# Down products by slot instead of by channel in the experts, and set keys summed from tail keys

## The chip, the cores and the metric

One NeuronCore of a Trainium2 chip runs the kernel. The metric is the device time of one execution in microseconds, the median of several. TensorE (PE) multiplies matrices, VectorE (DVE), ScalarE (ACT) and GpSimd (POOL) work on vectors, SyncE (SP) issues most transfers. A transfer that is indexed by rows, or that adds to memory, is issued by GpSimd.

## The reference

4096 tokens (4 x 1024) of 256 channels, all float32, pass through:

```python
x = x + 0.5 * ffn(layernorm(x))        # quantised kernel and a LoRA pair
x = x + set_attention(layernorm(x))    # below
x = x + 0.5 * ffn(layernorm(x))
x = x + 0.5 * moe(layernorm(x))        # below
x = x + linear_attention(layernorm(x))
x = x + 0.5 * moe(layernorm(x))
```

Set attention has 16 heads. Its keys are sums over dyadic sets of 4, 8, 16, ... tokens (512 sets with the padding of this kernel) and, for each query, the tail: the sum of the keys from the last multiple of four up to the query itself. Values are summed alike:

```python
K = k_cum[r_idx] - k_cum[l_idx - 1]           # sets of 4, 8, 16, ...
K_tail = k_cum[t] - k_cum[t - t % 4 - 1]      # 1 to 4 tokens
logits = [q @ K.T * scale (where t >= r_idx), sum(q * K_tail) * scale]
```

The MoE has 32 experts, each taking its 160 best tokens (slots) among those that have it in their top two, and 16 adapters, one for two experts:

```python
idx = argsort(-score, axis=0)[:160].T
gate, up = split(xf[idx] @ w_up.T)            # 2 x 512 of 256
ye = (silu(gate) * up) @ w_down.T             # 256 of 512
out = zeros.at[idx].add(w * ye)
# the adapter of the expert's pair: 2 x 128 of 256, then 256 of 128, times 0.05 * w
```

## The kernel before

The change touches two places: the front of the set attention, and the expert loops of both MoEs, which share their code (`moe1e`, `moe2e` in the names of tiles).

**Attention front** (`attention_front`, line 507). It works batch by batch. `tailT` holds the running sums of four tokens of the normalised x, made by GpSimd; `setT` holds the sums over the 512 sets, made by VectorE in `sets` by one reduction over four tokens and then level by level (L635 to L641). TensorE then runs, in this order: the queries (four groups), the turning of the next batch, the tail keys `u_kt` (four groups of 512), the tail values, the set keys `u_k` from `setT` (two groups of 512, L724 to L727), the set values `u_v`, and the logits of the tails `u_tl` from `prod`. VectorE multiplies tail keys by queries into `prod` (L666) and splits queries and keys into three bf16 parts each (`split`, L650 to L655), which SyncE writes to `q_parts` and `k_parts`. ScalarE brings every other bank out of PSUM, among them the set keys into `kT`.

**Experts** (`experts`, line 2201). Four experts are a quad, two quads a turn, four turns a MoE. The first two turns carry steps of the choice of tokens for the second half of the experts. A quad's 640 slots lie in five tiles of 128 rows: tile k for k < 4 has the first 128 slots of expert k, tile 4 the last 32 of all four. `ORDER` is the order in which TensorE, ScalarE and VectorE go through a turn; n counts its eight experts, i the five pairs of 128 gate and 128 up channels (four of the expert, one of the adapter):

- x: ten transposes of the gathered rows in three groups (`TWO`), each copied to `xgT` by ScalarE; up 0 waits for all three.
- up(n, i): four matmuls, weights stationary, 160 slots moving (L2383). ScalarE takes silu (L2436), VectorE the product into `h` (L2507), two experts deep.
- down(n), after up(n + 1): for each half of the channels five matmuls, `w_down` stationary and 160 slots of `h` moving (L2396). The result has channels on the partitions; ScalarE copies it to `yT` (L2443, L2444). All downs use bank 5.
- y: ten transposes turn `yT` to rows of slots (L2364), in three groups, those of the first quad among the ups of the next, the last two of the second quad at the turn's end. ScalarE multiplies by the slots' weights into `y` (L2462).

The profile counts each f32 matmul as two instructions; a transpose is one.

GpSimd gathers x of the quad after next (L1348) and then adds `y` to the token rows in memory (L2328). A token can be in two experts of a quad, but at most once per phase, so a quad is stored in two phases: five stores with `first`, a wait until they have landed, five with `second`. In the last quad tiles 0 and 1 are stored alone (`whole`), each landed before what follows; then three tiles in two phases.

SyncE loads the weights: `w_up[k]`, `w_down[k]` and adapters k // 2 have one buffer for each k of a quad. Expert n + 4's `w_up` is loaded after up(n), its `w_down` after down(n), an adapter pair's two tiles after the down of an odd n.

## Time and profile before

| | us |
|---|---|
| median of 3 runs (1768.47 to 1768.91) | 1768.47 |
| the profiled execution | 1774.75 |
| its span, first to last instruction | 1773.0 |
| TensorE busy (share of the span) | 1468.0 (83%) |
| VectorE, ScalarE, GpSimd busy | 975.0, 719.1, 563.5 |
| experts of MoE 1, TensorE: first up to last y | 805.2 to 1111.7 |
| experts of MoE 2, TensorE: first up to last y | 1443.5 to 1750 |
| attention front | 67 to 213 |
| mean granted TensorE clock | 0.905 |

Starts are in us from the span's start. [...]

### The profile page before, as it was taken

To read this page: it belongs to the slowest core of one execution; us is meant where nothing else is said; L and a number is where in the kernel's file an instruction comes from. 1 tells how busy PE (TensorE), PEld (TensorE's weight loads), DVE (VectorE), ACT (ScalarE), POOL (GpSimd) and SP (SyncE) were. 2 spreads that over 40 slices of the span, in tenths; PEclk is the share of its full clock that TensorE was granted. 3 is DMA by queue.
4 is the path that set the end of the run, shared out by engine and by line. 5 is a ranking of instruction groups with operands and counts; after the bars stand their busy time and mean duration, and the time that the engine had idled before them with its cause. 6 is when DMAs were issued, how large, how long until landed. Compare 5 with 4: busy or idle time off the path is not lost. (4 is left out here: it accounts for less than half of the span.)

```text
span 1773.0 us, 27014 instructions
## 1 busy us (share of the span) xinstructions
PE 1468.0 (83%) x9520; PEld 1131.4 (64%) x9520; DVE 975.0 (55%) x2816; ACT 719.1 (41%) x1744; POOL 563.5 (32%) x467
## 2 busy tenths in 40 slices
PE   6899979999999678438999999289895469999994
PEld 4566644555555455228889989166563349899994
DVE  8775577787875487874441111256675945521110
ACT  4223137666666377325523333004333435322331
POOL 6522120000000343303536563421211231636545
PEclk9989889999999899558999999699996569999997
DMA  3034373424220023314869995501113226979974
GB/s 105 18 119 127 109 123 65 91 42 93 42 47 2 1 84 107 140 31 151 246 183 261 239 241 133 137 20 48 48 43 135 72 79 205 228 230 232 267 194 46
DMA packets 113764, 212.10 MB, mean 120 GB/s; under 512 B 20101, under 2 KB 79658, under 8 KB 104426
## 3 DMA queue, kind: packets, MB, share of 16 engines
q1 hardware_dynamic: 87338, 178.93, 32.6%
q0 software_dynamic: 26304, 31.60, 11.6%
q8 instruction: 69, 1.13, 0.3%
q14 instruction: 53, 0.43, 0.1%
HBM read 158.71 MB, written 51.38 MB: 118 GB/s over the span
## 5 line engine op out<-in xcount | busy, mean ns | idle before, releaser
L952 DVE TENSOR_REDUCE attnm_top<-psum 128x1 f32<-128x384 f32 (+3 forms) x384 | 212.9, 597 | 59.8 <-PE psum L1037 55.7
L1174 ACT ACTIVATE attnm_prob<-psum 128x512 f32<-128x512 f32 (+1 forms) x384 | 192.1, 530 | 91.0 <-PE psum L1047 84.4
L2507 DVE SCALAR_TENSOR_TENSOR moe2e_h<-moe2e_gate,psum 128x160 f32<-128x160 f32 x160 | 50.4, 320 | 201.1 <-ACT moe2e_gate L2436 165.6
L2507 DVE SCALAR_TENSOR_TENSOR moe1e_h<-moe1e_gate,psum 128x160 f32<-128x160 f32 x160 | 50.4, 321 | 200.5 <-ACT moe1e_gate L2436 179.0
L2328 POOL DMA_INDIRECT x_sum<-moe1e_y,moe_scatter_i x76 | 119.4, 1571 | 129.4 <-ACT moe1e_y L2462 70.7
L2328 POOL DMA_INDIRECT out<-moe2e_y,moe_scatter_i x76 | 118.8, 1563 | 129.9 <-ACT moe2e_y L2462 69.8
L2383 PE MATMUL psum<-moe2e_xgT,moe_w_up 128*128 128x160 f32 x1024 | 152.3, 304 | 2.5 <-ACT moe2e_xgT L2452 1.9
L2383 PE MATMUL psum<-moe1e_xgT,moe_w_up 128*128 128x160 f32 x1024 | 152.4, 304 | 2.4 <-ACT moe1e_xgT L2452 1.9
L2383 PEld LDWEIGHTS psum<-moe2e_xgT,moe_w_up 128*128 128x128 f32 x1024 | 144.4, 193 | 4.8 <-issue 4.8
L2383 PEld LDWEIGHTS psum<-moe1e_xgT,moe_w_up 128*128 128x128 f32 x1024 | 144.4, 193 | 4.8 <-issue 4.8
L1348 POOL DMA_INDIRECT moe_xg<-xn_rows,moe_gather_i x80 | 83.9, 1049 | 159.2 <-DVE moe_gather_i L1536 93.0
L938 POOL TENSOR_TENSOR attnm_tail_v<-attnm_v_tail,attnm_tail_p 128x256 f32<-128x256 f32 x32 | 19.8, 620 | 346.5 <-PE psum L1089 284.5
L1035 PE MATMUL psum<-attn_mask_ts,ident_bf 128*128 128x128 bf16 x512 | 106.3, 227 | 9.1 <-DVE attnm_top L952 6.9
L1037 PE MATMUL psum<-attnm_k_hat,attnm_q_hat 96*128 96x512 bf16 (+3 forms) x384 | 107.4, 308 | 0.0
L1047 PE MATMUL psum<-attnm_q_hat,attnm_k_hat 99*128 99x512 bf16 (+1 forms) x288 | 98.4, 345 | 1.4 <-ACT attnm_prob L1174 0.6
L2436 ACT ACTIVATE moe1e_gate<-psum 128x160 f32<-128x160 f32 x160 | 47.2, 301 | 104.9 <-PE psum L2383 98.1
L2436 ACT ACTIVATE moe2e_gate<-psum 128x160 f32<-128x160 f32 x160 | 47.2, 301 | 104.9 <-PE psum L2383 92.2
L2396 PE MATMUL psum<-moe2e_h,moe_w_down 128*128 128x160 f32 x512 | 80.3, 300 | 2.1 <-ACT moe2e_yT L2444 1.2
L2396 PE MATMUL psum<-moe1e_h,moe_w_down 128*128 128x160 f32 x512 | 80.3, 300 | 2.1 <-issue 1.5
L1035 PEld LDWEIGHTS psum<-attn_mask_ts,ident_bf 128*128 128x128 bf16 x512 | 51.0, 101 | 46.2 <-issue 24.5
L1060 PE MATMUL psum<-attnm_prob,attn_v_aug 128*32 128x512 f32 (+1 forms) x768 | 78.7, 527 | 0.0
L1045 PE MATMUL psum<-attn_mask_st,ident_bf 128*128 128x256 bf16 x256 | 70.4, 277 | 5.4 <-DMA attn_q_first<-attnm_mT 5.3
(416 smaller groups left out, 3198.8 us busy)
## 6 DMA issues: line engine op xcount, KB each, us to landing
moe_w_up<-in_expert_up SPq DMA_DIRECT2D x64, 1024.0 KB
moe_w_down<-in_expert_down SPq DMA_DIRECT2D x64, 512.0 KB
attnm_q_hat<-q_parts SPq DMA_DIRECT2D x72, 128.0 KB, 4.7
moe_a_up<-in_adapter_up SPq DMA_DIRECT2D x32, 256.0 KB
q_parts<-attnf_q_part SPq DMA_DIRECT2D x12, 512.0 KB, 2.8
attnm_k_hat<-k_parts SPq DMA_DIRECT2D x72, 64.0 KB, 2.3
x_res<-in_x SPq DMA_DIRECT2D x8, 512.0 KB, 8.4
v_tails<-attnf_v_tail SPq DMA_DIRECT2D x4, 1024.0 KB, 4.3
```

The costliest lines, as they stand in the source:

```text
L952: nc.vector.tensor_reduce(top[:, n // QUADS % 2, tiles[0]:tiles[-1] + 1, hh:hh + 1], s.ps[:, u.bank, 0:len(tiles) * width].rearrange("p (t ...
L1035: nc.tensor.matmul(out[:, width - P:width], s.identb[:], o.mask_ts[:, tile % 2, :], start=(i == 0), stop=False, skip_group_check=True)
L1037: ins = nc.tensor.matmul(out, q_hat[r][0:MROW, h, tile * P:(tile + 1) * P], k_hat[r][0:MROW, h, 0:width], start=False, stop=True, skip_gro ...
L1047: nc.tensor.matmul(s.ps[:, u.bank, at:GROUP], k_hat[r][0:MROW + NPART, h, j * P:(j + 1) * P], q_hat[r][0:MROW + NPART, h, g * GROUP + at:( ...
L1060: ins = nc.tensor.matmul(s.ps[32 * h:32 * h + 32, u.bank, at:GROUP], o.v_aug[:, first:first + 32], prob[:, i % NPROB, at:GROUP], start=(j ...
L1174: nc.scalar.activation(prob[:, i % NPROB, at:GROUP], s.ps[:, u.bank, at:GROUP], ACT.Exp).then_inc(taken[u.bank], 1)
L1348: pool.indirect_dma_start(self.xg[:, q, k, :], None, self.rows, bass.IndirectOffsetOnAxis(ap=self.gather_i[:, at:at + 1], axis=0), bounds_ ...
L2328: nc.gpsimd.indirect_dma_start(total, bass.IndirectOffsetOnAxis(ap=rows, axis=0), y[:, q, k, :], None, bounds_check=TOKENS + SPARE - 1, oo ...
L2383: ins = nc.tensor.matmul(s.ps[:, u.bank, half * CAP:(half + 1) * CAP], lhsT, xgT[:, q, c, k * CAP:(k + 1) * CAP], start=(c == 0), stop=(c ...
L2396: ins = nc.tensor.matmul(s.ps[:, u.bank, o * CAP:(o + 1) * CAP], lhsT, h[:, n % 2, i, :], start=(i == 0), stop=(i == PAIRS - 1))
L2436: nc.scalar.activation(gate[:, i, :], s.ps[:, u.bank, 0:CAP], ACT.Silu).then_inc(silu, 1)
L2507: nc.vector.scalar_tensor_tensor(out=h[:, n % 2, i, :], in0=gate[:, i, :], scalar=1.0 if i < INTER // P else SCALE_A, in1=s.ps[:, u.bank, ...
```

## The change

*Front.* The product of the set keys is dropped. VectorE copies every fourth tail key, which is the sum of its four tokens, out of the PSUM bank from which it has just made `prod`, and builds the larger sets from these with the same additions as for `setT` (now the function `larger`).

*Experts.* The down product has the first 128 slots of `h` stationary and the 256 channels of `w_down` moving, five matmuls for an expert, and leaves rows of slots in PSUM; ScalarE weighs them at once into `y`. The last 32 slots of a quad's four experts are multiplied in `tails`, ahead of the quad's last down: 20 matmuls with 32 stationary columns each, expert k into partitions 32k to 32k + 31 of one bank. `yT` and its turns are gone; `h` is five experts deep. x comes in the groups (0, 4), (1, 2), (3), placed among the pairs of up 0. SyncE loads a quad's four `w_down` and two `a_down` after that quad's last down; `w_up` follows up(n), `a_up` its last pair. Quads 0 to 6 are stored in two phases as before; in the last one tiles 0, 1 and 2 are stored whole, each landed before the next, then the tail tile and tile 3 in two phases.

```diff
-                for f in range(CC):
-                    mm_group(u_k[b, f], [(s.ps[:, u_k[b, f].bank, :], lambda c: wk[:, c, f * P:(f + 1) * P],
-                                          lambda c: setT[:, z, c].rearrange("p j i -> p (j i)"))])
...
                         nc.vector.tensor_tensor(prod[:, f, g * GROUP:(g + 1) * GROUP], s.ps[:, u.bank, :],
-                                                qT[:, z, f, g * GROUP:(g + 1) * GROUP], ALU.mult).then_inc(taken[u.bank], 1)
+                                                qT[:, z, f, g * GROUP:(g + 1) * GROUP], ALU.mult)
+                        of_four = s.ps[:, u.bank, :].rearrange("p (j i k) -> p j i k", j=SC // BG, k=4)[:, :, :, 3]
+                        ins = nc.vector.tensor_copy(k_sets[:, f, g * SC // BG:(g + 1) * SC // BG, 0:64], of_four)
+                        ins.then_inc(taken[u.bank], 1)
+                v.wait_ge(taken[u.bank], u.after(0))
+                chain.link(larger(k_sets))
...
-TWO = [(0, 1), (2, 3), (4,)]
-ALONE = TWO[0]
+FETCH = [(0, 4), (1, 2), (3,)]
+TAIL = EQ
...
-    h = sb("h", [P, 2, PAIRS, CAP])
-    yT = sb("yT", [P, 2, CC, QE])
+    HELD = [0, 1, 2, 3, 4, 0, 1, 2]
+    h = sb("h", [P, EQ + 1, PAIRS, CAP])
...
         if n == 0:
-            ORDER += [("x", 0, None)] + [("up", 0, i) for i in range(PAIRS)]
+            ORDER += [("x", 0, 0)]
+            for i in range(PAIRS):
+                ORDER += [("up", 0, i)]
+                if i in (1, 3):
+                    ORDER += [("x", 0, (i + 1) // 2)]
         if n == 1:
-            ORDER += [("x", 1, None)]
+            ORDER += [("x", 1, i) for i in range(len(FETCH))]
         if n + 1 < 2 * EQ:
-            for i in range(PAIRS):
-                ORDER += [("up", n + 1, i)]
-                if n == EQ and i < len(TWO):
-                    ORDER += [("y", 0, i)]
-                if n == EQ + 2 and i == 0:
-                    ORDER += [("y", 1, 0)]
+            ORDER += [("up", n + 1, i) for i in range(PAIRS)]
+        if n % EQ == EQ - 1:
+            ORDER += [("tails", n // EQ, None)]
         ORDER += [("down", n, None)]
-    ORDER += [("y", 1, i) for i in range(1, len(TWO))]
...
+            def next_up(n):
+                if n < 2 * EQ and not (last and n >= EQ):
                     sp.wait_ge(full[u_up[n, INTER // P - 1].bank], up[n])
                     m.load_up(sp, t * 2 * EQ + n + EQ, n % EQ)
-                    sp.wait_ge(full[u_down[n].bank], down[n])
-                    m.load_down(sp, t * 2 * EQ + n + EQ, n % EQ)
                     if n % 2:
-                        m.load_adapter(sp, t * EQ + n // 2 + EQ // 2, n % EQ // 2)
+                        sp.wait_ge(full[u_up[n, PAIRS - 1].bank], a_up[n // 2])
+                        m.load_a_up(sp, t * EQ + n // 2 + EQ // 2, n % EQ // 2)
+
+            for q in range(2):
+                if last and q == 1:
+                    break
+                first = 0 if q == 0 else EQ + 2
+                for n in range(first, EQ * q + EQ):
+                    next_up(n)
+                sp.wait_ge(full[u_down[EQ * q + EQ - 1].bank], down[q])
+                for k in range(EQ):
+                    m.load_down(sp, t * 2 * EQ + EQ * q + EQ + k, k)
+                    if k % 2 == 0:
+                        m.load_a_down(sp, t * EQ + (q + 1) * EQ // 2 + k // 2, k // 2)
+                    if q == 0 and k % 2:
+                        next_up(EQ + k // 2)
...
+            else:
+                for k in range(EQ - 1):
+                    done = store(k, whole[k])
+                    landed(done)
+                for rows in (first, second):
+                    for k in (TAIL, EQ - 1):
+                        done = store(k, rows[k])
+                    if rows is first:
+                        landed(done)
...
+        def down_weight(k, i):
+            return w_down[k][:, i, :] if i < INTER // P else a_down[k // 2][:]
...
-            for o in range(CC):
-                for i in range(PAIRS):
-                    if o == 0:
-                        pe.wait_ge(taken[u_up[n, i].bank], u_up[n, i].after(t))
-                    lhsT = w_down[k][:, i, o * P:(o + 1) * P] if i < INTER // P else a_down[k // 2][:, o * P:(o + 1) * P]
-                    ins = nc.tensor.matmul(s.ps[:, u.bank, o * CAP:(o + 1) * CAP], lhsT, h[:, n % 2, i, :],
-                                           start=(i == 0), stop=(i == PAIRS - 1))
+            for i in range(PAIRS):
+                pe.wait_ge(taken[u_up[n, i].bank], u_up[n, i].after(t))
+                ins = nc.tensor.matmul(s.ps[:, u.bank, 0:C], h[:, HELD[n], i, 0:P], down_weight(k, i),
+                                       start=(i == 0), stop=(i == PAIRS - 1))
+            ins.then_inc(full[u.bank], 1)
+
+        def tails(t, q):
...
+            for i in range(PAIRS):
+                last = u_up[EQ * q + EQ - 1, i]
+                pe.wait_ge(taken[last.bank], last.after(t))
+                for k in range(EQ):
+                    rows = slice((CAP - P) * k, (CAP - P) * (k + 1))
+                    ins = nc.tensor.matmul(s.ps[rows, u.bank, 0:C], h[:, HELD[EQ * q + k], i, P:CAP], down_weight(k, i),
+                                           start=(i == 0), stop=(i == PAIRS - 1), skip_group_check=True)
```

The index list `whole` is now made for both halves of the experts (in `lists`, two VectorE operations more for the first half).

## Rows read from the trace of the kernel before

**Rows 1.** Windows in MoE 1: busy us by engine, clock, DMA share, GB/s.

```profile
949.00:1019.00 70.00, 66.98 (x481) 65.60 (x480) 12.55 (x41) 21.57 (x67) 41.51 (x30) 0.98 0.92 244
...
1111.70:1134.70 23.00, 0.02 (x1) 0.00 (x0) 0.00 (x0) 1.04 (x3) 10.87 (x7) 0.58 0.36 40
```

**Rows 2.** The chain that ended last, second MoE: start us, us, what.

```profile
1628.62 5.43 PE psum L2383 x40
1634.05 2.72 PE psum L2396 x20
...
1745.49 3.00 PE psum L2396 x20
```

**Rows 3.** Timeline of TensorE, MoE 1: start us, us, what, [idle before <-releaser].

```profile
1024.97 0.60 PE L2364 MATMUL psum<-ident,moe1e_yT 128*128 128x128 f32 x4
1025.41 3.42 PE L2383 MATMUL psum<-moe1e_xgT,moe_w_up 128*128 128x160 f32 x24
...
1033.22 1.35 PE L2396 MATMUL psum<-moe1e_h,moe_w_down 128*128 128x160 f32 x8 [0.58 <-issue]
...
1036.85 0.87 PE L2364 MATMUL psum<-ident,moe1e_yT 128*128 128x128 f32 x6 [0.65 <-ACT moe1e_yT L2444]
...
1038.43 1.09 PE L2354 MATMUL psum<-ident,moe_xg 128*128 128x128 f32 x8 [0.71 <-ACT moe1e_y L2462]
...
1040.74 4.47 PE L2383 MATMUL psum<-moe1e_xgT,moe_w_up 128*128 128x160 f32 x31 [0.54 <-issue]
```

**Rows 4.** Timeline of GpSimd: stores under load, a gather, the end of MoE 2.

```profile
1024.61 1.55 POOL L2328 DMA_INDIRECT x_sum<-moe1e_y,moe_scatter_i  x1 [5.47 <-DMA x_sum<-moe1e_y,moe_scatter_i]
...
1035.29 1.05 POOL L1348 DMA_INDIRECT moe_xg<-xn_rows,moe_gather_i  x1 [0.31 <-issue]
...
1746.38 1.55 POOL L2328 DMA_INDIRECT out<-moe2e_y,moe_c_whole  x1 [3.17 <-DMA out<-moe2e_y,moe_scatter_i]
...
1767.26 1.55 POOL L2328 DMA_INDIRECT out<-moe2e_y,moe_scatter_i  x1 [0.30 <-issue]
```

**Rows 5.** Timeline of TensorE in the attention front.

```profile
162.47 7.07 PE L689 MATMUL psum<-attnf_w,attnf_tailT 128*128 128x256 f32 x32
169.38 3.60 PE L689 MATMUL psum<-attnf_setT,attnf_w 128*128 128x512 f32 x8
172.81 3.62 PE L689 MATMUL psum<-attnf_w,attnf_setT 128*128 128x256 f32 x16
```

**Rows 6.** Timeline of VectorE in the attention front.

```profile
182.78 1.66 DVE L635 TENSOR_TENSOR attnf_setT<-attnf_setT 128x256 f32<-128x256 f32 x6
...
206.48 0.69 DVE L650 CAST attnf_k_part<-attnf_kT 128x1024 bf16<-128x1024 f32 x1 [7.40 <-issue]
```

**Rows 7.** Value products of attention: groups by shape, then timeline of TensorE.

```profile
L1060 PE MATMUL psum<-attnm_prob,attn_v_aug 128*32 128x256 f32 x8 | 0.6, 379 | 0.0
...
447.32 0.38 PE L1047 MATMUL psum<-attnm_q_hat,attnm_k_hat 99*128 99x512 bf16 x1
447.54 0.60 PE L1081 MATMUL psum<-ident,attnm_oT 128*128 128x128 f32 x4
...
448.25 0.38 PE L1047 MATMUL psum<-attnm_q_hat,attnm_k_hat 99*128 99x512 bf16 x1
448.56 1.50 PE L1060 MATMUL psum<-attnm_prob,attn_v_aug 128*32 128x512 f32 x16
449.99 0.23 PE L1035 MATMUL psum<-attn_mask_ts,ident_bf 128*128 128x128 bf16 x1
```

**Rows 8.** DMA issues by line, then timeline of SyncE.

```profile
attnf_w<-in_attn_wqkv SPq DMA_DIRECT2D x1, 768.0 KB, 4.2
...
1036.23 0.33 SPq L1356 DMA_DIRECT2D moe_w_down<-in_expert_down  x1
```

**Rows 9.** Timeline of TensorE at the start of MoE 1.

```profile
799.85 1.12 PE L2354 MATMUL psum<-ident,moe_xg 128*128 128x128 f32 x4 [7.66 <-DMA moe_xg<-xn_rows,moe_gather_i]
...
805.22 6.02 PE L2383 MATMUL psum<-moe1e_xgT,moe_w_up 128*128 128x160 f32 x32 [0.66 <-ACT moe1e_xgT L2452]
```

More of the change, by code:

```diff
@@ L2308, in gather @@
             m.gather(pool, quad)
+        stored = itertools.count(1)
         def add(quad):
             q, t = quad % 2, quad // 2
+            choice, at = m.choices[quad // late.quads], quad % late.quads
+            whole = [choice.whole[:, at, k:k + 1] for k in range(EQ)]
             first, second = ([scatter_i[:, (quad * 2 + i) * ST_TILES + k:(quad * 2 + i) * ST_TILES + k + 1]
                               for k in range(ST_TILES)] for i in range(2))
-            phases = [list(enumerate(first)), list(enumerate(second))]
@@ L2317, in add, with store @@
-            if quad == QUADS_E - 1:
-                phases = [[(k, late.whole[:, late.quads - 1, k:k + 1])] for k in ALONE] + [of[len(ALONE):] for of in phases]
+            def store(k, rows):
+                u = u_tails[q] if k == TAIL else u_down[EQ * q + k]
+                pool.wait_ge(taken[u.bank], u.after(t))
+                nc.gpsimd.indirect_dma_start(total, bass.IndirectOffsetOnAxis(ap=rows, axis=0),
+                                             y[:, q, k, :], None, bounds_check=TOKENS + SPARE - 1, oob_is_err=True,
+                                             compute_op=ALU.add).then_inc(y_out, 16)
+                return next(stored)
```

212 lines of the change are left out of this document (101 added, 111 removed).

## The prediction

> **What bounds the kernel now.** I read the views in this order. First the windows of the expert stages: over a middle turn (two quads of four experts) TensorE is busy 66.98 of 70 us at clock 0.98, while the DMA engines are busy for 0.92 of the time and VectorE and ScalarE for less than a third; then come 23 us without TensorE [rows 1]. Second the chain that ended last: through the second MoE it is TensorE group after group, one expert's up product (5.43 us, L2383) and its down product (2.72 us, L2396) in turn; TensorE leaves it at 1745.49 + 3.00 = 1748.5 us [rows 2]. So an expert costs 8.15 us of TensorE and whatever shortens that, or the gaps between, shortens the stage. Third TensorE's timeline at a boundary between turns: it turns y (L2364), then x (L2354), and sits idle 0.58, 0.65, 0.71 and 0.54 us in between, 2.5 us a turn [rows 3]. Fourth GpSimd at the end of a MoE, which alone sets those 23 us: the last store is issued 18.8 us after TensorE's last product [rows 2, 4]. Fifth the attention front, where TensorE runs group after group without a gap [rows 5]. DMA is the second resource: not yet waited for, but with little room.
>
> **The profiled execution** took 1774.75 us with a span of 1773.0; the median of the three timed runs is 1768.47, 0.3% less. Savings are taken over at their size in us.
>
> **Front: set keys from the tail keys.** Removed per batch: the product L724-727, 8 instructions of 512 columns, from 169.38 to 172.81, 3.43 us [rows 5]. TensorE is the bound there, so four batches give 13.7 us; should the group of one batch lie in a stretch at half clock, it is worth twice as much, so up to 17. Added to VectorE: four strided copies out of PSUM and nine small sums. The six sums of the same shape take 1.66 us, the other four some 0.5; a copy is under 0.3, as 0.69 us is already paid for a 1024-element cast: together 3.4 us. Its cover is the 7.40 us that VectorE idles ahead of the key split [rows 6]. It now need not wait for the product at all, so the split starts at about 202.7 instead of 206.48. If the cover were gone, 3.4 us a batch would come back. ScalarE's two evacuations vanish, at no gain. **Front: -13.7 us** (-12 to -17).
>
> **One turn of the experts.** A product of 128 slots by 256 channels in f32 costs what the 32 instructions from 162.47 to 169.38 do: 6.91/32 = 0.216 us each [rows 5]. A down product by slot is five matmuls, ten instructions, 2.16 us against 2.72. Eight experts: -4.5. The turns of y go: four transposes take 1025.41 - 1024.97 = 0.44 us [rows 3], ten a quad 1.1, two quads: -2.2. The tails come in: 20 matmuls a quad of 32 stationary columns by 256. One after the other they would take 40 x 0.216 = 8.6 us, four column groups side by side 2.16. The row that decides is the value product of the attention, with the same 128x32 weights and the same 256 columns: eight instructions are busy for 0.6 us where eight in a row would take 1.7, and sixteen (half of 512 columns) pass from 448.56 to 449.99, 1.43 us, against 1.28 for perfect overlap and 5.1 for none [rows 7]. I take 2.16, two quads: +4.3. Work: -2.4 us a turn, -9.4 a MoE, 0.6 of it behind the last product.
>
> The groups of 32 columns are entered and left twice a turn. Before the value product the matmul of L1047 is followed after 0.31 us, elsewhere after 0.22 (0.09 more), and 1.43 - 1.28 = 0.15 remain on the way out [rows 7]: 0.24 a visit, eight visits: +1.9 a MoE. [...]
>
> Gaps: at a boundary the waits for the copies of y, for their bank, and for bank 5 go, the last because the tails stand between down 6 and down 7. Left is the copy of the first x group, now two ScalarE copies: some 0.9 us, and 0.3 in the second x. 2.5 becomes 1.2: -1.3 a turn, -5.2 a MoE. Banks 6 and 7 and the h slots hold nothing up: the slot written by up 5 was last read by down 0 and the tails.
>
> **The wait that is added.** All four w_down of a quad are read by its tails, so SyncE can load none until the quad's last down product is through; before, each was loaded with three experts' time to spare. Queued behind that wait on SyncE are the four w_down, two a_down and the next w_up. At a turn's end the cover is x and two ups, over 11 us. In the middle of a turn it is one up, 5.43 us [rows 2]. To be landed by then: 640 KB. The nearest row is a 768 KB load that lands in 4.2 us with the queue to itself, and issue costs 0.33 us a transfer [rows 8]; 0.33 + 0.5 for the second issue + about 4 = 5 us, just covered. But stores run then on GpSimd's queue; a landing that takes 3.2 us when quiet takes 5.5 us under load [rows 4], 2.3 more. The bounds are 0 and 3 us of stall; I take 1.0. Four times: +4 (0 to +12) a MoE.
>
> **Start of a MoE.** x tiles 0 and 4 are gathered first, and up 0 waits for these alone. Now TensorE turns the first two tiles at 799.85 and starts up 0 at 805.22, with 0.66 us for a copy [rows 9]. Afterwards: 799.85 + 0.5 + two copies and their signals, about 802.0. The other groups have landed by the second pair. **-3.2 us.** Two added VectorE operations in `lists` come after the gather indices, while TensorE waits 7.66 us for the first x [rows 9]: 0.
>
> **End of a MoE.** A store costs 1.55 + 0.30 us, a landing wait 3.2 (quiet) to 5.5 us after it [rows 4]. Before, from the last down product to the landing: 1767.26 + 1.55 + 3.0 - 1748.5 = 23.3 us. Afterwards I count from E, the end of quad 6; TensorE ends at E + 5.43 x 3 + 2.16 x 5 = E + 27.1, plus the stall and drain, E + 28.3. GpSimd: tile 3 and the tail of quad 6, first phase, landed at E + 7.3; five stores, landed at 19.5; tiles 0, 1 and 2 whole, one after another at 4.7 each, 33.6; two stores and landing 40.2; again, 46.9. So 18.6 us after TensorE instead of 23.3, -4.7; with landings under load in quad 6 some 2.3 less. I take **-4.0**. GpSimd, not TensorE, sets this part: three landings in a row cost more than they save in stores, and a TensorE that is earlier by 1 us gains nothing in the last quad alone.
>
> GpSimd's cycle: ten stores 18.6, five gathers 1.36 each [rows 4] 6.8, a landing 3.2 to 5.5: 28.6 to 30.9 us against 33.6 for half a turn. It holds, and y of a parity is free about 14 us before ScalarE wants it.
>
> **Sum** per MoE: start -3.2, work -9.4 + 0.6 = -8.8, visits +1.9, gaps -5.2, weights +4.0, end -4.0: -15.3. Two: -30.6. With the front: -44.3. 1768.5 - 44.3 = **1724 us**.
>
> **Rivals.** (A) *The weights give it back.* Landing late by 3 us or more in mid-turn, or the bunched loads make transfers of the first experts late elsewhere. For it: DMA share 0.92 in the middle turn [rows 1]. Against: averaged over the turn the bytes don't grow, and one up covers the quiet price. At 3 us, +8 a MoE over my term: 1740; with the end not gaining either, 1748. Chance 0.17. [...] (B) *Slower: the tails don't overlap*, because four different w_down tiles are streamed. Each quad then pays 8.6 instead of 2.16, 6.5 x 16 = +104: 1828. It decides above 2.16 + 44.3/16 = 4.9 us a quad. Against: in the value product each group has a moving operand of its own too and overlaps [rows 7]. Chance 0.04. (C) *No stall, and the clock holds.* The middle turns show a stretch below full clock after a boundary (0.98 over 70 us [rows 1], 1.4 us); with shorter gaps it may go, and the weights land in time: -8 -3: 1713; with a front of 17 and a full -4.7 at the end, 1708. Chance 0.17. (D) *GpSimd becomes the bound of the stage*: a landing of 5.5 us in both phases, and the gathers slowed by the bursts; 3 us a quad over half a turn in ten quads: 1754. Chance 0.03. Forecast, with its stalls of 0.3 to 2 us: 0.59, 1716 to 1736.
>
> **Range**: from C's lower end, less 2 us for what C itself leaves open, to A with a lost end: 1706 to 1748. A measurement of this kernel can tell 0.2% (3.5 us) from no change. Faster 0.95 (forecast, A, C, most of D), same 0.01, slower 0.04 (B).
>
> **What would show it.** Right: in the front no 512-column group of the set keys, and TensorE's period per batch 3.4 us less; down groups of ten instructions in 2.16 us; the tails' 40 instructions in 2.2 to 2.5 us; turns, from the first up product to the next turn's, shorter by 2.5 to 3.5 us; a gap on TensorE ahead of the first down product of a turn's second quad, released by the w_down load, of 0 to 2 us, and none ahead of other downs; three landings in a row in the last quad, and the last store issued about 14 us after TensorE's last product. Wrong: tails of 4 us or more (B), that gap over 3 us or gaps at other downs (A), GpSimd without an idle microsecond over a turn (D), or the key split on VectorE later than the products of TensorE that follow it.

## The result, and the profile of the changed kernel

The changed kernel took 1743.94 us (median of 4, 1737.69 to 1750.05), the kernel before beside it 1768.69 us (1768.47 to 1771.16): ratio 0.9861, interval 0.9833 to 0.9889, so 24.7 us or 1.4% faster. The forecast was 1724, 44.3 us faster. On three further occasions the same kernel took 1728.7, 1740.5 and 1724.5 us (below): how much it gains depends on the occasion, which the kernel before does not show.

**What came as told.** Timeline of TensorE in the changed kernel, end of the middle turn in MoE 2 and start of the next (start us, us, line, tiles, rows*columns, count, [idle before <-releaser]):

```profile
1627.77 1.67 PE L2427 MATMUL psum<-moe_w_down,moe2e_h 128*128 128x256 f32 x7
1629.28 0.59 PE L2427 MATMUL psum<-moe_a_down,moe2e_h 128*128 128x256 f32 x2
1629.80 1.93 PE L2441 MATMUL psum<-moe_w_down,moe2e_h 128*32 128x256 f32 x32
1631.55 0.61 PE L2441 MATMUL psum<-moe_a_down,moe2e_h 128*32 128x256 f32 x8
1632.10 1.99 PE L2427 MATMUL psum<-moe_w_down,moe2e_h 128*128 128x256 f32 x8
1633.93 0.59 PE L2427 MATMUL psum<-moe_a_down,moe2e_h 128*128 128x256 f32 x2
1634.36 0.60 PE L2394 MATMUL psum<-ident,moe_xg 128*128 128x128 f32 x4
1640.16 4.63 PE L2413 MATMUL psum<-moe2e_xgT,moe_w_up 128*128 128x160 f32 x16 [5.20 <-ACT moe2e_xgT L2490]
```

A down product passes in some 2.2 us (1632.10 to 1634.36 with the return from the column groups) where it took 2.72 [rows 2]. A listed duration can reach past the start of the group behind it (1631.55 + 0.61 = 1632.16, and the next starts at 1632.10), so I read paces from starts. The tails' 40 instructions pass in 2.30 us (1629.80 to 1632.10), 0.14 more than the 2.16 of four groups side by side: the groups overlap almost in full. Nothing of y is turned any more [rows 3].

**What came otherwise** is in the last row. TensorE idles 5.20 us before the first up of the turn, where I had counted on some 0.9. ScalarE and GpSimd in the same stretch:

```profile
1629.91 0.47 ACT L2501 ACTIVATE moe2e_y<-psum,moe2e_weight 128x256 f32<-128x256 f32 x1 [1.86 <-PE psum L2427]
1635.01 0.47 ACT L2501 ACTIVATE moe2e_y<-psum,moe2e_weight 128x256 f32<-128x256 f32 x1 [4.62 <-remote]
1637.91 0.47 ACT L2501 ACTIVATE moe2e_y<-psum,moe2e_weight 128x256 f32<-128x256 f32 x1 [2.43 <-remote]
1639.38 0.37 ACT L2492 COPY moe2e_xgT<-psum 128x256 f32<-128x256 f32 x1 [1.00 <-remote]
```

```profile
1629.99 1.09 POOL L1348 DMA_INDIRECT moe_xg<-xn_rows,moe_gather_i  x1 [0.31 <-issue]
...
1635.38 1.01 POOL L1348 DMA_INDIRECT moe_xg<-xn_rows,moe_gather_i  x1 [0.30 <-issue]
1636.69 1.62 POOL L2344 DMA_INDIRECT out<-moe2e_y,moe_scatter_i  x1 [0.30 <-issue]
```

By TensorE's records the tails were through at 1632.1, the last down at 1634.4 and the x turn at 1634.8. ScalarE, which did nothing else, took them up at 1635.01, 1637.91 and 1639.38: 2.9, 3.5 and 4.6 us later. The releaser is listed as "remote", the profile's word where no recorded instruction fits the signal. I call this a **late signal**. The profile's ends of TensorE's instructions are modelled, so the rows do not tell whether the signal was late or the product behind it. It falls in or just after the five gathers of GpSimd (1629.99 to 1636.39). The gap has a second price, in the windows of the same kernel (span, busy us of TensorE, its weight loads, VectorE, ScalarE, GpSimd; clock, DMA share, GB/s):

```profile
1632.00:1636.00 4.00, 2.96 (x18) 2.32 (x14) 0.00 (x0) 0.47 (x1) 3.09 (x4) 1.00 0.88 219
1636.00:1640.00 4.00, 0.00 (x0) 0.00 (x0) 0.00 (x0) 1.09 (x3) 3.39 (x3) 0.92 0.52 97
1640.00:1644.00 4.00, 3.84 (x14) 3.85 (x15) 0.32 (x1) 0.33 (x2) 3.31 (x3) 0.50 1.06 351
1644.00:1648.00 4.00, 4.00 (x24) 3.96 (x24) 0.64 (x2) 1.25 (x4) 1.55 (x1) 0.72 1.11 303
```

After the idle stretch the granted clock is 0.50 in each window of 2 us from 1640 to 1646, and 0.95 in the next: the first 16 up instructions are busy for 4.63 us instead of 2.44 (the same 16 at a granted clock of 1.00 on occasion D, below). Such a stretch at 0.50 is what I call half clock. So 4.4 us more of gap come with some 3 us more of work behind it.

The waits of ScalarE that end on "remote" add up to 51 us in the two MoEs of this profile (21 waits); in the kernel before they are 3.7 us (2 waits of 1.85). Most cost nothing, as TensorE runs on meanwhile. Those at a turn's start cost the gaps of 4.66 us (at 1485.57), 5.20 us (1640.16) and 2.00 us (1008.43). Beside them there are two stalls on `a_down`, 1.28 and 0.65 us; my term for the weights had 4 us a MoE.

One table goes through all that follows. From the timelines of TensorE I took for each MoE the stretch from the first x turn to the end of the last down product; from ScalarE's the sum of its waits on "remote"; the times are the medians. "Occasion" names the runs that were made side by side; B and D were made on one chip, C on another.

| Run | occasion | median us | profiled us | MoE 1 | MoE 2 | late signals, us | longest gap at a turn's start |
|---|---|---|---|---|---|---|---|
| before | A | 1768.7 | 1774.8 | 311.9 | 312.0 | 3.7 | 0.8 |
| changed | A | 1743.9 | 1737.7 | 295.7 | 308.3 | 51 | 5.20 |
| changed | B | 1728.7 | 1740.9 | 299.2 | 302.3 | 30 | 3.72 |
| changed | C | 1740.5 | 1741.9 | 302.0 | 302.1 | 41 | 5.24 |
| changed | D | 1724.5 | 1724.1 | 292.3 | 292.1 | 0 | 0.81 |

(In the kernel before, the stretch ends with the last turn of y, 1.5 us behind the last product.) The three profiles with late signals have stretches that sum to 601.5 to 604.1 us and took 1737.7 to 1741.9; the one without has 584.4 and took 1724.1. On occasion B only the profiled execution was so long; the other five took 1724.8 to 1729.5 us. A profile shows one execution, and a median is that of several, so times and stretches are best compared within the profiled executions.

### The profile page after: what moved, and what is told of

The parts are those of the page before. It is cut to its first block and busy times, and to the rows that moved or that the text cites. A ratio compares the mean times of both kernels' runs of the same rounds, so it can differ in the third digit from the quotient of the medians.

```text
span 1736.0 us, 26631 instructions
## 1 busy us (share of the span) xinstructions
PE 1433.7 (83%) x9328; PEld 1075.2 (62%) x9328; DVE 988.1 (57%) x2872; ACT 689.3 (40%) x1640; POOL 561.6 (32%) x465
## 5 line engine op out<-in xcount | busy, mean ns | idle before, releaser
L2413 PE MATMUL psum<-moe2e_xgT,moe_w_up 128*128 128x160 f32 x1024 | 154.3, 309 | 11.5 <-ACT moe2e_xgT L2490 6.0
L2413 PEld LDWEIGHTS psum<-moe2e_xgT,moe_w_up 128*128 128x128 f32 x1024 | 148.5, 197 | 14.8 <-issue 13.9
L87 DVE BATCH_NORM_STATS2 x_stats<-x_res 128x6 f32<-128x256 f32 x128 | 44.5, 412 | 36.1 <-DMA x_res<-x_sum 35.5
L2427 PE MATMUL psum<-moe_w_down,moe2e_h 128*128 128x256 f32 x256 | 62.1, 384 | 1.5 <-issue 0.9
```

What stands on the lines that cost most here:

```text
L2413: ins = nc.tensor.matmul(s.ps[:, u.bank, half * CAP:(half + 1) * CAP], lhsT, xgT[:, q, c, k * CAP:(k + 1) * CAP], start=(c == 0), stop=(c ...
L2427: ins = nc.tensor.matmul(s.ps[:, u.bank, 0:C], h[:, HELD[n], i, 0:P], down_weight(k, i), start=(i == 0), stop=(i == PAIRS - 1))
```

## The experiments

The runs are told in the order of the questions.

**The changed kernel again**, on occasion B, unedited.

> The changed kernel once more, beside the parts of it. In its first profile ScalarE waited 49.9 us in all for signals of TensorE that came 2 to 6 us after TensorE's own records of the products ended (3.8 us in the kernel before). If these late signals are what spreads its times (1737.7 to 1750.1), the time is 1738 to 1750 again, and an execution with more of them is a longer one. If they belong to that one profile only, the time is within 2 us of 1744 and this profile shows under 10 us of them.

Measured: 1728.72 us (1724.83 to 1740.85), ratio 0.978 (0.9762 to 0.9798). Neither of the two outcomes came. The one profiled execution, with 30 us of late signals, is the longest of the six.

**The front alone**, with the experts as before.

```
-        for f in range(CC):
-            u_k[b, f] = use()
...
+                chain.link(larger(k_sets))
```

> Only the front of the change, on the kernel before. My working gave -13.7 us (four groups of 3.43 us of TensorE), so 1755. If VectorE's added sums took the place of the product, or the clock's slow stretches moved, the gain is under 8 us, 1761 or more.

Measured: 1755.71 us (1751.51 to 1760.45), ratio 0.993 (0.9909 to 0.9951), beside 1768.25: -12.5 us, against -13.7. The 512-column group is gone, as TensorE's timeline of this run shows (it ran from 169.38 to 172.81 [rows 5]):

```profile
174.37 7.03 PE L696 MATMUL psum<-attnf_tailT,attnf_w 128*128 128x512 f32 x16
181.23 7.07 PE L696 MATMUL psum<-attnf_w,attnf_tailT 128*128 128x256 f32 x32
188.14 3.62 PE L696 MATMUL psum<-attnf_w,attnf_setT 128*128 128x256 f32 x16
191.59 3.63 PE L742 MATMUL psum<-attn_head_sum,attnf_prod 128*128 128x8 f32 x32
```

**The experts alone**, with the front as before (the rest of the diff).

> Only the experts' part. By my working -30.6 us (1738). By the first profile, in which the first MoE gained 14.8 us and the second 2.0 us and the end of neither MoE gained, it is 1750 to 1760. If front and experts add up, this gain and that of the front alone give the whole change's.

Measured: 1750.09 us (1739.12 to 1753.79), ratio 0.9904 (0.9886 to 0.9922): -18.2 us, against -30.6. The two parts give -30.7 together, the whole gave -39.5 on this occasion; 9 us are not additive, and why is not shown: this profile has 32 us of late signals, a gap of 5.12 us at 1643.02 and MoE stretches of 293.3 and 300.6 us, but it is that of the fastest of the seven executions (1739.12; the others took 1747.7 to 1753.8).

**The gather between the two phases of a quad**, in the wait for the landing of the first phase, so that no gather runs under the tails.

```
                     if rows is first:
+                        ahead(quad)
                         landed(done)
...
-            if quad + 2 < QUADS_E:
-                gather(quad + 2)
             add(quad)
```

> The changed kernel with one move: GpSimd issues the five gathers of the quad after next between the two phases of stores, inside the wait for the first phase's landing (8.3 to 9.8 us in middle turns), instead of ahead of the stores. Theory (gathers under way while the tails run hold TensorE's signals back, and GpSimd's backlog of 6.8 us a quad sets the end): no tails product overlaps a gather any more, late signals fall from 50 us to under 15, the first whole store of the last quad is no longer late, and the time falls by 8 to 16 us, to 1728 to 1736. Rival (the signals are late because of the bunched weight loads, or it is the landing of the stores alone that sets the end): late signals stay above 30 us and the time moves by less than 4 us.

Measured: 1765.43 us (1760.2 to 1773.26), ratio 0.9983, 37 us slower than the changed kernel beside it. The profile has no late signal, and something worse: TensorE waits for x at three turn starts of each MoE.

```profile
880.18 2.77 PE L2397 MATMUL psum<-ident,moe_xg 128*128 128x128 f32 x10 [4.82 <-DMA moe_xg<-xn_rows,moe_gather_i]
```

The others are 5.65, 6.51, 5.27, 4.32 and 4.75 us, each with a stretch of lower clock behind it (0.50 to 0.52 in its lowest window of 2 us); the MoE stretches are 312.6 and 312.3 us, 20 more than at the changed kernel's best. The cause is GpSimd's queue: the five gathers, now behind the quad's first five stores, ran from 871.41 to 878.04, and TensorE stood waiting from 875.36 on. I had held GpSimd to be free for 3 to 5 us in a quad. In the changed kernel (occasion D) GpSimd's waits for a landing were this long in a middle turn:

```profile
960.65 1.56 POOL L2344 DMA_INDIRECT x_sum<-moe1e_y,moe_scatter_i  x1 [3.72 <-DMA x_sum<-moe1e_y,moe_scatter_i]
...
994.49 1.55 POOL L2344 DMA_INDIRECT x_sum<-moe1e_y,moe_scatter_i  x1 [8.71 <-DMA x_sum<-moe1e_y,moe_scatter_i]
```

From one set of gathers to the next it is 28.9 and 33.8 us (941.11, 969.97, 1003.79): 25.4 us of stores and gathers, and a landing. A quad of TensorE takes 35.3. GpSimd is nearly full, as rival D had it, and just not the bound. The two waits differ although the DMA engines are as busy in both (share 1.07 and 1.08): in the shorter one they move 226 GB/s and in the longer one 348, behind the bunched `w_down` loads that SyncE issues from 978.86 on.

**The changed kernel, a third time** (occasion C), beside the three runs that follow.

> The changed kernel as it is, for the three that run beside it on the same chip. It gave 1743.9 us once and 1728.7 us on another occasion, with late signals of TensorE adding up to 50 and 30 us of waits. If these waits set the difference, the sum of the waits that end on a remote releaser in this profile goes with its time: about 30 us at 1725 to 1741 us, about 50 us at 1738 to 1750 us. If they are no cause, the time is anywhere in 1725 to 1750 us whatever the sum of these waits.

Measured: 1740.49 us (1738.58 to 1751.92), ratio 0.9858 (0.9812 to 0.9904), 41 us of late signals, and one gap of 5.24 us (1015.92) and one of 4.50 (1645.43). Behind the first the granted clock is 0.50 from 1015 to 1021, behind the second 0.50 from 1647 to 1649.

**Alternating kinds.** Every expert slot holds the first or the second pick of its token, so first picks never meet each other's rows, nor second picks theirs; only the two kinds must be kept apart. Odd quads therefore store their second picks first. The landing between quads goes, one a quad stays, and the gathers fill it. `free` waits for the other quad's stores and hands its y back. (The spare rows that empty slots are added to get a second set, and each parity of quads gets a semaphore of its own.)

```
-            landed(done)
...
-                for rows in (first, second):
+                for i, rows in enumerate((first, second) if q == 0 else (second, first)):
                     for k in range(ST_TILES):
+                        if i == 0 and k == ST_TILES - 1:
+                            free()
...
+                    if i == 0:
+                        ahead(quad)
+                        landed(q)
```

> Odd quads store second picks first and then first picks, so that the last phase of a quad and the first one of the next add rows of one kind and no landing lies between them; the gather for the quad after next stands between the two phases, in the landing wait, as in the run with the moved gather. Theory that GpSimd bounds the loaded turns: its work per quad was 10 stores of 1.86 us, 5 gathers of 1.35 us and a landing wait of 8.9 us, 34.3 us of a turn of some 35.5 us; now it is 18.6 + 6.8 + about 2 = 27.4 us. GpSimd then idles for some 5 to 8 us per quad until ScalarE has weighed a tile, x is there at every turn (no wait of 4 to 6 us as with the moved gather alone), the second to last quad's stores end before TensorE's last product and not 2 us after it, and the end from the last product to the last landing shrinks from 23.3 to about 20 us: 5 to 15 us faster than the changed kernel. Rival, GpSimd is beside the path all the time: GpSimd idles more, everything else stays, within 3 us of the changed kernel. Rival, a gather between the phases is bad for whatever reason: 15 us or more slower, as the moved gather alone was (+37 us).

Measured: 1731.80 us (1724.37 to 1734.92), ratio 0.9803 (0.9776 to 0.983), 8.7 us faster than the changed kernel beside it, within the 5 to 15 expected, and none of its five executions (up to 1734.92) is as long as the shortest of the changed kernel's four (1738.58). GpSimd now waits for work (timeline, MoE 1):

```profile
1027.14 1.55 POOL L2352 DMA_INDIRECT x_sum<-moe1e_y,moe_scatter_i  x1 [0.30 <-issue]
1033.09 1.55 POOL L2352 DMA_INDIRECT x_sum<-moe1e_y,moe_scatter_i  x1 [4.40 <-ACT moe1e_y L2509]
1040.68 1.55 POOL L2352 DMA_INDIRECT x_sum<-moe1e_y,moe_scatter_i  x1 [6.04 <-ACT moe1e_y L2509]
```

Late signals are 15 us, the gaps at turn starts 1.2 to 2.45 us (a little of x's lateness stays), and the stretches are 294.5 and 294.8 us against 302.0 and 302.1. The end did not shrink, against the expectation: the last store is issued 18.9 us after the last product. Nor does this run show a gain where there are no late signals: the stretches are 2.2 and 2.7 us longer than those of the changed kernel on occasion D.

**A quarter of the up weights**: is it the load of the transfers? The reloads bring 256 KB of each expert's 1 MB and leave the rest as it was, so the results are others.

```
-                    m.load_up(sp, t * 2 * EQ + n + EQ, n % EQ)
+                    m.load_part(sp, t * 2 * EQ + n + EQ, n % EQ)
...
+        sp.dma_start(self.w_up[k][:, :, 0:INTER // 2], self.drams[0][bass.ds(e, 1), :, :, 0:INTER // 2].rearrange(
+            "o p c j -> (o p) c j")).then_inc(self.up_in[k], 16)
```

> Every expert's up weights after the first quad are reloaded only in a quarter of their columns (256 KB and not 1 MB each), so that stale weights are used and the output is another; instructions and their order stay. Theory that the transfers' load makes stores land late and signals come late: landing waits in the middle turns fall from 8 to 10 us to the 3.1 us of the quiet end, no wait of ScalarE ends on a remote releaser for more than 1 us, and the time falls by 10 to 25 us against the changed kernel. Rival, the five gathers themselves hold the signals up: landing waits fall, but late signals of 2 to 6 us stay at the gathers, and the time falls by less than 10 us.

Measured: 1751.82 us (one execution), within the 1738.58 to 1751.92 of the changed kernel beside it; a fall by 10 to 25 us, which the theory asked for, did not come. Over 940 to 1010 the DMA share falls to 0.76 and 172 GB/s. The landing waits between two phases do not fall to the 3.1 us that I expected: they are 3.6 and 8.0 us in this stretch and 6.5 us in the mean of all 14 (3.6 to 9.9), against 7.6 us (3.7 to 10.0) in the changed kernel beside it. The late signals are 60 us (27 waits, up to 7.1) where they were 41, and four turns start with gaps of 4.74 to 5.57 us. So the bytes of the up weights account for a small part of the landings, and they are not what makes the signals late.

**Ten whole products in place of the tails**: is it the column groups?

```
-                for k in range(EQ):
-                    rows = slice((CAP - P) * k, (CAP - P) * (k + 1))
-                    ins = nc.tensor.matmul(s.ps[rows, u.bank, 0:C], h[:, HELD[EQ * q + k], i, P:CAP], down_weight(k, i),
+                for k in (EQ - 1,):
+                    ins = nc.tensor.matmul(s.ps[:, u.bank, 0:C], h[:, HELD[EQ * q + k], i, 0:P], down_weight(k, i),
```

> The tails of a quad, 40 products of 32 rows in four column groups (2.3 us), are replaced by one expert's 10 products of 128 rows (2.2 us), so the tail tile holds wrong rows. Theory that TensorE's column groups hold its own signals up: no late signal at the tails any more, TensorE's gaps at turn starts fall to 0.8 us, and the time falls by 5 to 15 us against the changed kernel. Rival, the late signals come from GpSimd's or the transfers' side: they stay at 20 us or more in all, and the time stays within 3 us of the changed kernel.

Measured: 1722.59 us (1719.15 to 1728.68), ratio 0.9752 (0.9717 to 0.9788): 18 us faster than the changed kernel beside it, a little more than the 5 to 15 expected. The stretches are 291.1 and 290.8 us, late signals 17 us, and no gap over 1.8 us; behind the turn start at 1006.67, with a gap of 0.81 us, the granted clock stays at 1.00 up to 1020. That is what the theory asked for. But the tails themselves took 2.3 us where these products take 2.2, so the 18 us are not time of the array; they are the gaps and the clock behind them.

**Forty products of 64 columns on the whole array**: is it the groups, or the number of instructions?

```
+                    cols = slice(C // EQ * k, C // EQ * (k + 1))
+                    ins = nc.tensor.matmul(s.ps[:, u.bank, cols], h[:, HELD[EQ * q + k], i, 0:P], down_weight(k, i)[:, cols],
```

> The tails' 40 products of 32 rows in four column groups become 40 products of 128 rows and 64 columns on the whole array, which last about as long (2.2 us), so the tail tile holds wrong rows. The run with 10 products of 128 rows and 256 columns had no gap of over 2 us at a turn start and was 18 us faster than the changed kernel. Theory that column groups hold the signals up: this run is like that one, no gap of over 2 us, 15 us or more faster than the changed kernel beside it. Rival, the number of instructions does (40 products and 40 weight loads in 2.3 us against 10 and 10): gaps of 4 to 5 us at one turn start in each MoE stay, with a stretch at half clock behind them, and the time is within 5 us of the changed kernel.

Measured: 1749.12 us (1746.84 to 1753.14), ratio 0.9885 (0.986 to 0.991). It is 24.6 us slower than the changed kernel beside it, which neither the theory nor the rival had, and it answers another question than mine (TensorE, then its weight loads):

```profile
1008.54 3.68 PE L2441 MATMUL psum<-moe_w_down,moe1e_h 128*128 128x64 f32 x32
1012.05 1.06 PE L2441 MATMUL psum<-moe_a_down,moe1e_h 128*128 128x64 f32 x8
1012.95 1.95 PE L2427 MATMUL psum<-moe_w_down,moe1e_h 128*128 128x256 f32 x8
```

```profile
1008.32 3.76 PEld L2441 LDWEIGHTS psum<-moe_w_down,moe1e_h 128*128 128x128 f32 x32
```

The 40 products pass in 4.41 us, 0.110 each, not in 2.2. The stream alone would take 0.054 each by my estimate, a quarter of 0.216, while the weight loads, one for each product, are busy without a break. So I take it that they set the pace; no run separates the two. That is 2.1 us a quad and 16.9 a MoE, and the stretches, 308.7 and 308.1 us, are 16.4 and 16.0 longer than those of the changed kernel beside it. The profile has no late signal, but neither has the changed kernel's on this occasion, so it does not decide between the groups and the number of instructions.

**The changed kernel, a fourth time** (occasion D).

> The changed kernel as it is, for those that run beside it. With one gap of 4 to 5 us at a turn start in each MoE and the half clock behind it, 1735 to 1745 us; with such a gap in one MoE or none, 1722 to 1732 us.

Measured: 1724.51 us (1720.04 to 1727.4), ratio 0.9737 (0.971 to 0.9763), and in its profile no wait on "remote" at all. The end of a middle turn again, in MoE 1, first TensorE and then ScalarE:

```profile
1004.87 1.99 PE L2427 MATMUL psum<-moe_w_down,moe1e_h 128*128 128x256 f32 x8
1006.70 0.59 PE L2427 MATMUL psum<-moe_a_down,moe1e_h 128*128 128x256 f32 x2
1007.13 0.60 PE L2394 MATMUL psum<-ident,moe_xg 128*128 128x128 f32 x4
1008.54 2.44 PE L2413 MATMUL psum<-moe1e_xgT,moe_w_up 128*128 128x160 f32 x16 [0.81 <-ACT moe1e_xgT L2490]
```

```profile
1007.33 0.47 ACT L2501 ACTIVATE moe1e_y<-psum,moe1e_weight 128x256 f32<-128x256 f32 x1 [1.85 <-PE psum L2427]
```

The gathers start under the tails as on occasion A (at 1003.79; the tails run from 1002.57 to 1004.87), and the signals are on time: ScalarE has the last down 0.2 us after its end. The turn's first 16 up instructions take 2.44 us, at a granted clock of 1.00. So the meeting of gathers and tails is not enough for a late signal.

**All eight quads in two kinds**, the run with alternating kinds plus this edit: the last quad loses its three whole tiles, each landed before the next.

```
-            if quad < QUADS_E - 1:
-                for i, rows in enumerate((first, second) if q == 0 else (second, first)):
-                    for k in range(ST_TILES):
+            for i, rows in enumerate((first, second) if q == 0 else (second, first)):
+                for k in (0, 1, 2, TAIL, EQ - 1):
...
-            else:
-                free()
-                for k in range(EQ - 1):
-                    store(k, whole[k])
-                    landed(q)
```

> As the run with alternating kinds and the gather between the phases, and the last quad is stored like the others, in its two kinds, in place of three tiles with all their rows and a landing wait of 3.0 us after each. Theory that the end is bounded by GpSimd's work and not by TensorE's last product: after the second phase of the quad before (its last store began at 1068.07) come 10 stores of 1.86 us and two landings of 3.1 us, 24.8 us, so the last landing is at about 1094.7 in MoE 1 and not at 1100.4: 5 to 6 us per MoE, 10 to 12 us in all against the run without this edit, 1720 us beside its 1731.8. Rival, the stores of a phase that waits for the last tile are late themselves (a landing under load of 6.5 us): no more than 3 us per MoE.

Measured: **1713.01 us** (1711.05 to 1718.3), ratio 0.9673 (0.9652 to 0.9693), beside 1771.8; 11.5 us less than the changed kernel beside it. Timeline of GpSimd from TensorE's last product on (it ends at 1079.6):

```profile
1079.48 1.55 POOL L2352 DMA_INDIRECT x_sum<-moe1e_y,moe_scatter_i  x1 [1.73 <-issue]
1081.33 1.55 POOL L2352 DMA_INDIRECT x_sum<-moe1e_y,moe_scatter_i  x1 [0.30 <-issue]
1086.23 1.55 POOL L2352 DMA_INDIRECT x_sum<-moe1e_y,moe_scatter_i  x1 [3.35 <-issue]
...
1093.64 1.55 POOL L2352 DMA_INDIRECT x_sum<-moe1e_y,moe_scatter_i  x1 [0.30 <-issue]
```

The last store is issued 14.1 us after that product instead of 18.6 (1095.53 - 1076.9): 4.5 us a MoE, 9.1 of the 11.5. The stretches are 290.6 and 293.2 us against 292.3 and 292.1: here, with no late signal in either profile, the alternation itself gives nothing that can be told apart.

**The same once more**, on a chip of its own.

> The kernel with all eight quads stored in two alternating kinds, once more. The changed kernel took 1724.5, 1728.7, 1740.5 and 1743.9 us on four occasions; its profile without a late signal of TensorE is that of 1724.5, the others had 30 to 50 us of waits that end so. If the placing of the gathers between the phases keeps such signals away from the tails and the turn of x, this kernel stays within 5 us of its 1713.0 us here too, with no gap of over 3 us at a turn start, whatever the occasion. Rival, the first time was a quiet occasion: late signals of 2 to 6 us at the gathers, gaps of 4 to 5 us at turn starts and 1720 to 1732 us.

Measured: 1721.10 us (1719.23 to 1723.89), ratio 0.9737 (0.9724 to 0.9751), beside 1767.6. Eight us slower than the first time, so the rival is right that this was a quiet occasion; late signals are back with 23 us (14 waits, up to 3.3). They stay off the turn starts, though: the longest gap there is 2.13 us, the stretches are 293.8 and 295.2, and the last store is issued 14.3 us after the last product. The changed kernel did not run on this occasion. Against the kernel before beside it, this one gains 46.5 us, more than the changed kernel did on occasions A, B and C (24.7, 39.5 and 28.4) and as much as it did on D (47.3); the theory's "within 5 us of its 1713.0" did not hold.

## Why the prediction was right, and where it was wrong

The sign and the range held: 1743.9 lies in 1706 to 1748. That is luck in part, as it lies near rival A's value and for another reason, which no rival had. Of the 44.3 us forecast the median gained 24.7. The profiled execution (1737.69) gained 31.0 and can be taken apart: the ends of the MoEs gave nothing where I had 8.0 us, the two stretches gave 19.9 us (16.2 and 3.7) where I had 23.8, and the front was 1.2 short. Two steps failed there. One is "tile 3 and the tail of quad 6, first phase, landed at E + 7.3", of the end (below). The other is "Left is the copy of the first x group, now two ScalarE copies: some 0.9 us", of the gaps: the copy takes that, but ScalarE had to wait for TensorE's signals first, and three turns started with gaps of 4.66, 5.20 and 2.00 us. Behind the two long ones came a stretch at half clock (0.50 from 1486 to 1489 and from 1640 to 1646); behind the short one the clock was 1.00 from 1008 on. Against the 292.3 and 292.1 us of occasion D the stretches are 19.6 us longer; that they come within 4 us of my sum is because other terms were too dear.

The forecast of 1724 is what the kernel does on a quiet occasion (1724.5). Even there it is the sum of errors that cancel. Point by point, with the changed kernel of occasion D against the kernel before:

- **Front**, -13.7: -12.5 by the run of it alone. Right. VectorE's six sums took 1.66 us, as in the row of the same shape [rows 6], in two batches and 2.4 in the other two, under the same cover.
- **Start of a MoE**, -3.2: the first up comes 1.90 us after the first x turn (784.65, 786.55), before 5.37 [rows 9]: -3.5. Right.
- **Work, tails and visits**, -2.4 and +0.5 a turn: by the rows -4.5 for eight downs, -2.2 for y, +4.6 for two tails of 2.30 with their switches, -2.1. Right. Rival B is dead. A visit to the column groups costs 0.14 us (2.30 - 2.16), where I had 0.24.
- **Gaps**, -1.3 a turn: 3.0 us of idle in the old turn, from 962.76 to 1038.43, and 1.1 in the new one without the weights: -2.0. Right on D; on occasion A this is the step that failed.
- **Weights**, +4.0 a MoE: mis-sized. One stall of 0.8 us in MoE 1 and one of 0.7 in MoE 2; 1.9 us in both together on occasion A and again on C, one of 2.3 on B. With 3.2 us a MoE too much, this is the largest error in the stretch. The loads that all wait for the last down product land under one up product in nearly all cases, as they would at the 4.2 us of the row [rows 8], without the 2.3 us that I added for load.
- **The clock**, left out of the sum and given to rival C: in the kernel before, the stretch from 962 to 970 had a granted clock of 0.79, which cost 1.7 us. With shorter gaps the turn from 936.45 to 1007.13 has 1.00, and it shrank from 75.67 to 70.68 us. But the other middle turns of the kernel before have 1.00 throughout; only the third turn of each MoE has such a stretch. So this is 1.7 us a MoE, 2.0 with what the first turn's start saves.
- **End of a MoE**, -4.0: wrong, it gave nothing. From the last product to the issue of the last store it was 18.8 us [rows 2, 4] and is 18.6. The step that failed is "tile 3 and the tail of quad 6, first phase, landed at E + 7.3". E is 1049.36 (occasion D), and these are the rows:

```profile
1052.65 1.55 POOL L2344 DMA_INDIRECT x_sum<-moe1e_y,moe_scatter_i  x1 [0.31 <-issue]
1060.90 1.55 POOL L2344 DMA_INDIRECT x_sum<-moe1e_y,moe_scatter_i  x1 [6.69 <-DMA x_sum<-moe1e_y,moe_scatter_i]
...
1072.89 1.55 POOL L2344 DMA_INDIRECT x_sum<-moe1e_y,moe_c_whole  x1 [2.99 <-ACT moe1e_y L2501]
...
1095.53 1.55 POOL L2344 DMA_INDIRECT x_sum<-moe1e_y,moe_scatter_i  x1 [0.30 <-issue]
```

Landed at E + 11.5, as a landing waits 6.7 us here and not 3.2, and the stores before it begin later than I had them. All that follows is 4 us late, and my count of 18.6 to the last landing becomes 23.2 (1095.53 + 1.55 + 3.0 - 1076.9), against 23.3 before. No run shows the drain that stands beside the stall in "E + 28.3"; the last product was through at E + 27.5. In the kernel before, a landing at this place waited 3.04 us. These are the windows of the two waits, first before, then changed (span, busy us of TensorE, its weight loads, VectorE, ScalarE, GpSimd; clock, DMA share, GB/s):

```profile
1092.95:1095.99 3.04, 3.04 (x25) 3.04 (x24) 0.92 (x3) 0.91 (x3) 0.01 (x1) 1.00 0.37 43
1054.21:1060.90 6.69, 6.69 (x46) 6.43 (x45) 1.44 (x5) 1.69 (x5) 0.00 (x1) 1.00 0.83 259
```

The last quad's `w_down` loads, which the change moved behind the last down product of quad 6, are issued from 1049.55 on and are under way in the second window. I took the price of a quiet landing for a place to which the change had moved transfers. The sentence "GpSimd, not TensorE, sets this part" was right, and the run with all quads in two kinds shows it: other stores, the same TensorE, 4.5 us.
- **GpSimd's cycle**, 28.6 to 30.9 us: 28.9 and 33.8, with landings of 3.7 and 8.7 (5.5 assumed). A landing waited 3.04 us in the window above at 43 GB/s and 6.69 us in that at 259. The stores on GpSimd's queue paid more than the weights did (a landing of 8.7 us where I had 5.5, stalls on the weights of 0.8 and 0.7 us), and rival A had the weights pay.

The terms up to the end of the stretch were -11.9 a MoE; the rows give -19.6 in MoE 1 on occasion D (3.2 of the difference from the weights, 2.0 from the clock, the rest from start, work, visits and gaps together) and -16.2 and -3.7 on occasion A. To the last landing it was -15.3, and is 315.4 - 333.7 = -18.3 on D. Two of these and the front's 12.5 make 49.1 us; D measured 47.3 (1771.8 - 1724.5).

**Between 1724 and 1744** lie the late signals. On the quiet occasion the two stretches of TensorE sum to 584.4 us; on occasions B and C they are 17.1 and 19.7 us longer, and the profiled executions are longer by 16.8 and 17.8. On occasion A they are 19.6 us longer and the profiled execution only 13.6, as the parts outside the stretches took 6 us less. What is shown: 121 of the 127 late signals in the profiles above fall in or within 4 us behind a run of gathers (the other six within 5.7 us), and the two of the kernel before are among them, 3.0 us behind; they fill gaps at a turn's start only where ScalarE's x copy stands behind a weighing that waits for one; a gap of 5 us costs a stretch at half clock besides (0.50 for 6 us behind the 5.20 us on occasion A and behind the 5.24 on C); with fewer bytes in flight they do not go; and three profiles with another order or without the tails' column groups have late signals but no gap of over 2.5 us at a turn's start (two of alternating kinds with the gathers between the phases, one of whole products), two of them beside a changed kernel that has gaps of 5.24 and 4.50. What stays open is why TensorE's signal is late (or its product), whether the column groups or the number of instructions have a part in it, and why it comes on one occasion and not on another, on the same chip too (B and D): the profile names no releaser, and the kernel before has hardly any. The runs without a single late signal on occasion D (three kernels) are no evidence for their edits.

## What to carry to other kernels

Price a landing at the load that the changed stage will have, not at the row that is nearest in kind: here 3.0 us quiet, 6.7 behind the loads that the change had moved, and 8.7 in a middle turn, all for the same store. Before an engine's queue is given more to do or another order, add up its cycle with these waits; and where accumulating stores wait for one another, ask which rows can meet at all: that let landings go, and it gave 4.5 us at the end of each MoE, where GpSimd sets the time. If a gain differs by 1% between occasions while the kernel before does not move, count the waits that end on no recorded instruction before trusting any one profile.

## What the runs showed of the hardware

- Late signals, changed kernel on occasion A: ScalarE took up the tails, the last down and the x turn 2.9, 3.5 and 4.6 us after TensorE's records of them had ended, and SyncE issued the w_down load that waits for the last down at 1637.90, 3.5 us after its record's end and with ScalarE's 1637.91. Whether the signal or the work is late is open. All such waits of ScalarE add up to 51 us there, to none on occasion D, and to 60 us in the one profile with the up weights cut to a quarter, against 41 in the changed kernel beside it.
- The granted clock behind a gap of TensorE at a turn's start, changed kernel: 0.50 for 6 us behind 5.20 us (occasion A) and 5.24 us (C), 1.00 behind 2.00 us (A) and 0.81 us (D). Sixteen up instructions were busy for 4.63 us behind the 5.20 and for 2.44 behind the 0.81.
- Forty products of 32 rows by 256 columns in four column groups: 2.30 us (changed kernel, A and D). Forty of 128 rows by 64 columns on the whole array: 4.41 us, 0.110 each (the run with forty such products). Ten of 128 by 256: 2.16 us (1000.94 to 1003.10 in the run with ten whole products).
- The wait for a store's landing: 3.0 us in the end of MoE 1 in the kernel before (43 GB/s); in the changed kernel on occasion D 6.7 us at 259 GB/s, 3.7 us at 226 and 8.7 at 348, the last two at a DMA share of 1.07 and 1.08. With a quarter of the up weights the mean of 14 waits was 6.5 us, against 7.6 in the changed kernel beside it.
